# Two transfers of a last attention head issued from two engines, gate weights' low parts moved back, one statistic later

## The reference

```python
x = layernorm(x + attn(x, wq, wk, wv, wo))          # rope, causal softmax, 1024 tokens, width 512
nx = x * rsqrt(mean(x * x) + 1e-5) * ln_w
x = layernorm(x + (silu(nx @ gate.T) * (nx @ up.T)) @ down.T)
```

## Time and profile before

| | |
|---|---|
| time, 3 runs | 1129.82 us median (1127.23 to 1130.62) |
| the profiled execution | 1127.58 us, span 1125.8 us |
| mean granted clock of TensorE | 0.994 |
| busy: PE, DVE, POOL, ACT | 98%, 79%, 76%, 58% of the span |

### The profile page before, as it was taken

The page is one execution under the profiler, slowest core; times in us unless marked ns, Lnnn a source line. Parts: engine busy times, 40 slices in busy tenths (PEclk is TensorE's granted clock), DMA queues, the critical chain, the costliest instruction groups (busy, mean ns, idle before and its releaser), DMA issues.

```text
span 1125.8 us, 19197 instructions
## 1 busy us (share of the span) xinstructions
PE 1097.9 (98%) x5310; PEld 930.9 (83%) x5310; DVE 888.6 (79%) x1530; ACT 647.5 (58%) x1165; POOL 858.1 (76%) x583
## 2 busy tenths in 40 slices
PE   8899999999999999999999999999999899999997
PEld 6788888888888888888888888888877787888886
DVE  6777888778877887778788878878887898866767
ACT  5656666666666666656666666666665564333333
POOL 1799789978997899789879977998887658444431
PEclk9899999999999999999999999999999999999999
DMA  7856556555555555556556655565554502111102
GB/s 214 223 141 154 136 139 158 130 146 145 152 132 140 140 149 131 142 148 162 135 146 153 158 135 144 150 163 138 144 130 115 159 20 74 58 57 56 37 19 75
DMA packets 155550, 144.86 MB, mean 129 GB/s; under 512 B 15488, under 2 KB 135808, under 8 KB 155520
## 3 DMA queue, kind: packets, MB, share of 16 engines
q1 hardware_dynamic: 143360, 124.57, 42.8%
q10 hardware_dynamic: 12160, 19.93, 6.2%
HBM read 37.49 MB, written 2.10 MB: 35 GB/s over the span
## 4 chain that ended last, share of the span: by engine, by line
PE 38%; POOL 35%; issue 17%; DVE 3%; DMA 2%; ACT 2%; SPq 1%; ACTq 1%; POOLq 1%; DVEq 0%
POOL qk_raw L566 8%; PE ACC L1562 8%; POOL PT_lo L592 8%; PE ACC L1564 8%; PE ACC L1563 8%; POOL rope_s L567 6%; POOL Q_lo L576 4%; PE S L1562 4%; PE S L1564 3%; PE S L1563 3%; POOL wq_lo L545 2%; POOL wo_lo L545 2%; POOL qk_raw L570 2%; PE S L1578 2%; PE S L1580 1%
## 5 line engine op out<-in xcount | busy, mean ns | idle before, releaser
L1138 DVE CUSTOM_DVE_ANT_0 S<-S,mask 128x128 f32<-128x128 f32 (+7 forms) x256 | 194.1, 758 | 153.3 <-PE S L1580 153.3
L772 ACT ACTIVATE probs<-S,neg_max 128x128 f32<-128x128 f32 (+7 forms) x256 | 189.4, 740 | 191.8 <-DVE neg_max L1138 190.0
L592 POOL TENSOR_TENSOR PT_lo<-PT_lo,PT_hi 128x896 fp32r<-128x896 f32 (+1 forms) x90 | 199.9, 2221 | 21.4 <-ACT PT_hi L779 21.3
L1151 DVE STREAM_TRANSPOSE turned<-probs 128x128 f32<-128x128 f32 (+7 forms) x256 | 197.6, 772 | 2.0 <-ACT probs L772 2.0
L1221 DVE SCALAR_TENSOR_TENSOR y<-ACC,row_rcp,y 128x512 f32<-128x512 f32 x256 | 176.4, 727 | 1.6 <-PE ACC L1564 1.5
L566 POOL TENSOR_TENSOR qk_raw<-qk_raw,cos_sin 128x512 f32<-128x512 f32 x76 | 126.2, 1661 | 64.5 <-DMA rope_s<-qk_raw 64.2
L779 ACT ACTIVATE PT_hi<-PT_lo 128x896 fp32r<-128x896 f32 (+3 forms) x155 | 157.1, 1013 | 30.4 <-DMA PT_lo<-turned 30.3
L1578 PE MATMUL S<-K_hi,Q_hi 128*128 (+4 forms) x380 | 131.0, 345 | 3.2 <-ACT probs L772 2.4
L1562 PE MATMUL ACC<-PT_hi,V_hi 128*128 128x512 f32 (+1 forms) x378 | 129.8, 343 | 4.4 <-POOL PT_lo L592 3.0
L1563 PE MATMUL ACC<-PT_lo,V_hi 128*128 128x512 f32 (+1 forms) x378 | 131.0, 347 | 0.0
L1564 PE MATMUL ACC<-PT_hi,V_lo 128*128 128x512 f32 (+1 forms) x378 | 130.7, 346 | 0.0
(11 more groups left out here) (265 smaller groups left out, 2576.8 us busy)
## 6 DMA issues: line engine op xcount, KB each, us to landing
PT_lo<-turned SPq DMA_DIRECT2D x248, 112.0 KB, 2.5
PT_lo<-turned SPq DMA_DIRECT2D x124, 208.0 KB, 4.1
rope_s<-qk_raw ACTq DMA_DIRECT2D x152, 128.0 KB, 3.6
PT_lo<-turned SPq DMA_DIRECT2D x124, 128.0 KB, 2.6
PT_lo<-turned SPq DMA_DIRECT2D x124, 80.0 KB, 2.2
wq_raw<-in_L_attn_wq_dram SPq DMA_DIRECT2D x32, 256.0 KB, 2.8
wo_raw<-in_L_attn_wo_dram SPq DMA_DIRECT2D x32, 256.0 KB, 3.8
V_stage<-in_L_ffn_down_w_t_dram SPq DMA_DIRECT2D x7, 512.0 KB, 3.3
```

The lines of the kernel that those rows point to most:

```text
L592: nc.gpsimd.tensor_tensor(lo, lo.bitcast(F32), hi.bitcast(F32), ALU.subtract).then_inc(pt_lo_done[half], 1)
L772: nc.scalar.activation(dst, src, ACT.Exp, bias=neg_max[:, at:at + 1], scale=-1.0, accum_out=row_sum[:, j % 2, i:i + 1]).then_inc(exp_done, 1)
L1138: nc.vector.tensor_tensor_reduce(src, src, bias, scale=1.0, scalar=MASKED, op0=ALU.add, op1=ALU.min, accum_out=neg_max[:, at:at + 1]).then ...
L1151: nc.vector.transpose(dst.rearrange("p b (r i) -> p r b i", i=QB), src.rearrange("p (r b i) -> p r b i", b=4, i=QB)).then_inc(turn_done, 1)
```

## The change

For the last head, SyncE issues only the block rows 0 and 1 of tiles 6 and 7 (k = 3 and 4; "tiles 7 and 8", counted from one); ScalarE issues rows 2 and 3 itself, behind a wait for the transposed tile. ScalarE's list gets another order: both `weight_high_first` come later. GpSimd waits for `last_lo_done` ahead of the weights' low parts. `statistics(2)` moves from behind the last `add_rows` of the loop to just ahead of `statistics(3)`.

```diff
-            def turn_over(k, dest=PT_lo):
+            def turn_over(k, dest=PT_lo, blocks=range(4)):
...
-                for a in range(4):
+                for a in blocks:
...
-                        turn_over(k, sources(j)[1])
+                        turn_over(k, sources(j)[1], range(2 if j == REP - 1 and k > 2 else 4))
...
             for k in (2, 3):
                 late_low(k, REP - 1)
+            pool.wait_ge(last_lo_done, 1)
             for k in range(2):
                 weight_low(k, gate_raw[:, 2 * k:2 * k + 2].rearrange("p a b -> p (a b)"),
...
+            def turn_over(k):
+
+                tile = SENT[k][0]
+                act_e.wait_ge(turn_done, HEADS * NT - NT + tile + 1)
+                cols = slice(tile % HT * PITCH[1] * QB, (tile % HT * PITCH[1] + tile + 1) * QB)
+                for a in (2, 3):
+                    src = turned[1][a * QB:(a + 1) * QB, :, cols]
+                    nc.scalar.dma_start(late_PT[1][1][:, a, cols].bitcast(F32), src).then_inc(pt_in[k], 16)
+
+            turn_over(3)
+            late_high(2, REP - 1)
+            turn_over(4)
+            piece_high(1)
             weight_high_first(0)
-            late_high(2, REP - 1)
-            weight_high_first(1)
-            piece_high(1)
             late_high(3, REP - 1)
             deviations(0)
             late_high(4, REP - 1)
             act_e.wait_ge(ln_w_in, 16)
             piece_high(0)
+            weight_high_first(1)
             piece_high(1)
...
-                    if j == REP - 1 and t:
+                    if j == REP - 1 and t in (1, 2):
                         statistics(t - 1, n["y"] - 1)
...
+            statistics(HT - 2, rows_0 - 1)
             statistics(HT - 1, rows_0)
```

## The result

Over 20 runs each the changed kernel takes 1130.47 us (1128.18 to 1132.08) and the kernel before 1128.62 us (1127.17 to 1130.91). The ratio is 1.0015, 95% interval 1.0009 to 1.0021: slower by 1.7 us by the ratio, 1.85 by the medians. The three runs of before shown ahead of the prediction had a median of 1129.82, 1.2 us above that of the 20.

The account below looks back on a forecast made before the run. TensorE, busy nearly everywhere, was bound locally by waits for tile 7 and the norms. +0.45 and +1.1 (clock) made +1.5 on 1127.58, 1129.1; half of 1.2 for the low profiled run gave 1129.7 us, range 1126.4 to 1132.4.

Parts of the forecast that it names:

- The sum: Last-head stage through the transposes: +0.45 us without the clock, +1.1 for it, +1.5 in all (bounds +0.2 and +2.2).
- the point: Whole kernel: forecast time 1129.7 us, from 1129.1 plus half of the 1.2 us between profiled time and mean.
- The range: Whole kernel: 1126.4 to 1132.4 us, with 0.86 for the same within about 0.3% (3.4 us).
- The two engines' taking of turns: VectorE and GpSimd on SBUF: one waits for the other's whole operation; tile 7's low part 1.2 us, both_norm(3) 1.2 later.
- rival (1): Norms beside GpSimd's weight work: not held up, transposes end near 897.2, -1.5 us, 1126.1 or 1127.3; chance 0.2.
- The clock: TensorE's gap before the second tile's transposes: clock falls with chance 6 in 10, costing 0 to 1.7 us, taken as 1.1.
- lands near 887.3, 2.0 us earlier: Tile 7's last transfer: issued near 884.65 through the split between SyncE and ScalarE, landing 2.67 us later.
- Rival (3): Tile 7's transfers: share the same DMA engines, may land as late as 889.3; same time as forecast, chance 0.05.
- rival (2): ScalarE's list: its own issues of up to 1.55 us delay piece_high(1); +1.9, with clock +3.0, 1130.6 or 1131.8; chance 0.25.
- a path I had called covered by 2 us: ScalarE's late high parts to GpSimd's tiles: an overrun moves only the last piece's other input, with 2 us to spare.
- The statistic: VectorE ahead of the aggregates: one more statistic, 0.6 us net, makes deviations(0) and late_high(4, 3) later.

Follow-up runs that it names:

- e4: Changed kernel, with GpSimd's up weights' low part also waiting for both_norm(3); ratio to before 0.9991 (0.9982 to 1.0001).
- e2: Changed kernel with the statistic of y tile 2 back in its old place; ratio to before 1.0015 (1.0004 to 1.0027).
- e9: Changed kernel, statistic back, up weights behind both_norm(3), deviations(0) behind late_high(4, 3), down weights' load behind the last head's transfers; ratio to before 0.9991.
- f2: Kernel before with one GpSimd wait added: up weights' low part behind both_norm(3); ratio to before 0.9988 (0.9974 to 1.0001).
- f1: Changed kernel again, word for word, for a second profile; ratio to before 1.0017 (1.0008 to 1.0027).
- e6: Changed kernel with the statistic back in its old place and the up weights' low part behind both_norm(3); ratio to before 0.9988 (0.9979 to 0.9997).
- e3: Kernel before with only GpSimd's wait for the last low part added; ratio to before 1.0004 (0.9993 to 1.0015).
- e10: Kernel before with two GpSimd waits: gate weights behind the last low part, up weights behind both_norm(3); ratio to before 0.9982 (0.9972 to 0.9991).
- e1: Changed kernel without GpSimd's wait for the last low part; ratio to before 1.0006 (0.9995 to 1.0017).

## Why the prediction was right or wrong

**The sum and the point.** The sum of the steps was +1.5 us against the profiled execution; the stage shows +1.8 and the timed runs +1.7 (by the ratio). But the point, 1129.7, lies 0.12 us under the median of before that it would be compared with, so as a forecast it said "no slower", and that was wrong: the interval excludes it. The step that failed is the base. I added 0.6 us, half the distance from the profiled time to the mean of four, and called the rest a clock fall that might be in my sum already. The profiled execution lay 1.04 us under the median of 20 runs, not 0.6, and the three runs' median 1.2 above it. A change adds to the kernel's median, not to a mixture of one low execution and a mean; by 20 runs the base was 1128.62, and with +1.5 the point 1130.1. A size of 1.5 us needs a base that is known better than three runs spread over 3.4 us give it. The range held the time, and "the same within 0.3%" was right.

**Steps, in us of the stage** (predicted, measured in after): `piece_high(1)` 3.87, 3.97; `deviations(0)` 7.79, 7.90; `late_high(4, 3)` 8.17, 8.30; low part of tile 7 ends 10.47, 10.60; last piece starts 10.62, 10.74; `both_norm(1)` ends 15.97, 15.99; `both_norm(3)` ends 16.92, 16.90. The 0.1 us in most comes from `piece_high(1)`, that is from ScalarE's issues. The two engines' taking of turns, read from four rows of before, carried all of it. The prediction's wording, large VectorE operations in SBUF, is too wide: in before a statistic of 128x512 took 0.68 us in the middle of GpSimd's low parts and wasn't held. By the Trainium skill, page "SBUF — State Buffer", section "SBUF: two separate sides", whichever of the two starts first has the shared ports for its whole instruction. The trace agrees: 0.52 us against 2.10 for the same norm in e4 and after. That also refutes rival (1), the norms not held up, which one sentence of the prediction calls the second.

**The clock.** Priced at 1.1 us with 6 in 10. It fell in both profiles of the changed kernel, and a fall costs 20.44 - 18.95 = 1.5 us there. Without it the sum said +0.45, and e2's stage, whose norms end as in after, gives 18.95 - 18.65 = +0.3. In before it falls too, on the last piece, where it costs about 0.9: 18.65 against 15.71 + 2.04 = 17.75, an estimate from the 2.04 us of the other profiles. The sum set the full price against nothing for before, rightly, since before's own time holds its 0.9. From `both_norm(3)` to the gate it is 2.94 us in before and 3.54 in after: 0.6 of the 1.8 us is the clock, 1.2 is the norms. That is a split of two profiles. In how many of the timed executions the clock fell isn't known: e2 has after's ratio of 1.0015 and a profile without a fall. So the agreement of +1.5 with +1.7 doesn't test the clock's price, and is in part luck.

**The transfers.** The step "lands near 887.3, 2.0 us earlier" was wrong. I had put the last issue forward and kept the 2.67 us of landing, without asking what SyncE issues next: the down weights, 512 KB, whose issue moved forward by 2.0 us too and into tile 7's transfers. In after the last issue starts at 3.03 us and tile 7 is in at 7.55, 4.5 us later; that is 0.2 us earlier than in before, not 2.0. Rival (3), the split doesn't hasten the landing, is right in effect. Its reason is shown in part: with the down weights held back (e9) the landing takes 3.45 us, and why that isn't 2.67 is open. It cost nothing, as said, since ScalarE came to tile 7 only at 8.3 us.

**ScalarE held by its issues**, rival (2). The second issue took 1.49 to 1.91 us in seven of ten profiles with the split and 0.79 or 0.80 in three. GpSimd's tile 6 then ends at 9.4 to 9.8 us instead of 8.6. I had priced it through `piece_high(1)`; it came through `late_high(2, 3)` and GpSimd, a path I had called covered by 2 us. With all issues on SyncE one of tile 6's is as long (1.11 us in before, 1.63 in f2; see the last section), but there it only delays later transfers; the split put it in front of ScalarE's work. In the changed kernel the statistic hides it (f1: tile 6 at 9.43, ScalarE's high part not ready before 9.32); with the statistic back it eats the whole 0.6 us (e2).

**The statistic.** +0.6 us on `deviations(0)`, as said. That its return would be a gain by itself, as I expected of e2, was wrong, for the reason just given; in e6, with ScalarE's issues short and the norms free, the stage was 1.0 us shorter than in e4, of which some is e4's late transfer of tiles 4 and 5.

## What to carry to other kernels

When an operation is moved out of the way of one wait, list what runs where it lands: GpSimd's 5 us of low parts held VectorE's one low part by 0.8 us and a norm by 0.35, and moved behind the low part they held that norm by 1.6 us. A queue freed early isn't idle; its next transfer starts early too and may run among the ones that were to be hastened. And a forecast smaller than the spread of the runs should be stated as a difference, with the point put on the best-known median.

## What the runs showed of the hardware that I had not expected

- One issue among tile 6's four takes long, whoever makes it. With the split SyncE's four kept to 0.54 to 0.62 us and ScalarE's second took 0.79 or 1.5 to 1.9 us. With SyncE alone its third took 1.11 us in before, 0.95 in e3, 1.61 in e10 and 1.63 in f2, the others 0.54 to 0.62. So it isn't two engines issuing at once, nor ScalarE. Why is open. In e10 and f2 tile 7 then also landed half a microsecond later than in before.

```profile
882.85 1.11 SPq L411 DMA_DIRECT2D xT_lo<-turned  x1
```

- VectorE's and GpSimd's turns go by who starts first, to 0.04 us (e1): the loser, GpSimd, took 2.33 us for 1.29 us of work.
- The stage begins between 881.4 and 884.9 us in fourteen profiles of kernels whose code before it is the same. In before and after the difference arises early: one of TensorE's waits for x's low parts ends at 14.57 and at 15.97 us. Behind the stage the fourteen profiles agree within 0.3 us, so the part ahead of the stage spreads by 3.4 us, about as much as the stage itself differs between the kernels (16.77 to 20.44 us).
